# Ternary feed-forward of a fused transformer kernel: transposes moved from TensorE to transposing DMAs, row maxima and rounding two tiles ahead

## The chip, the cores and the metric

The kernel runs on one core of a Trainium2 chip. The metric is the device time of one launch in microseconds (us). The core has a matrix engine (TensorE, PE in the profile), a vector engine (VectorE, DVE), an activation engine (ScalarE, ACT), a general engine (GpSimd, POOL) and a queue that only issues transfers here (SyncE, SP). Each engine runs its own program in order and waits on semaphores.

## The reference, cut to what matters

The whole function is two transformer layers: attention and a ternary feed-forward, then a long convolution and an 8-bit feed-forward. The change touches the ternary feed-forward of layer 0. On the normalised rows `x` (2048 rows of 512) it computes

```python
def _quant_weight(w):
    scale = jnp.mean(jnp.abs(w)) + EPS
    return jnp.clip(jnp.round(w / scale), -1.0, 1.0) * scale
def _quant_act(x):
    scale = jnp.maximum(jnp.max(jnp.abs(x), axis=-1, keepdims=True), EPS) / 127.0
    return jnp.clip(jnp.round(x / scale), -128.0, 127.0) * scale
gate = sigmoid(bitlinear(x, w_gate))      # 512 -> 2048
up = bitlinear(x, w_up)                   # 512 -> 2048
return bitlinear(gate * up, w_down)       # 2048 -> 512
```

where `bitlinear(x, w)` is `_quant_act(x) @ _quant_weight(w).T`. Each row is thus scaled by its own maximum and rounded to whole numbers, once before the first two products and once before the third. The result, times a gate, is added to the residual.

## The kernel before, in words

`phase_bitlinear` (line 880) is one block of the program. It works on 16 tiles of 128 rows, in a loop that is unrolled by `over_tiles`. The weights already lie in memory as bfloat16 whole numbers. A tile `t` goes through these steps:

1. DVE, `prepare` (lines 1063 to 1073): centre and scale the row (`xn`), take its maximum, form the scale and its inverse, multiply and add MAGIC (which rounds), form the gate and up scales, subtract MAGIC into `xq` (bfloat16). This is done for tile t+1 while tile t is worked on.
2. PE, `turn_x` (line 942): four 128x128 transposes of `xq` into PSUM. ACT, `copy_x` (line 998): the copy from PSUM to `xT`.
3. PE, line 976: for each of four chunks c of 512 hidden columns, 4 matmuls for gate and 4 for up, into one of two PSUM buffers `G`. Chunk c waits until the product of chunk c-2 is formed (`h_ready`).
4. ACT, line 1031: sigmoid of the gate half. DVE, line 1123: times the up half, into `h`. DVE, line 1097 (`chunk_max`): the maximum of the chunk.
5. DVE, `quantise` (lines 1086 to 1092), at the head of the next tile: the row's maximum and scales, then `h` times scale plus MAGIC over all 2048 columns. ACT, `round_h` (line 1012): minus MAGIC into `hq` (bfloat16), behind the sigmoid of chunk 1.
6. PE, `turn_h` (line 953): sixteen transposes of `hq`, behind chunk 3 of the next tile. ACT, `copy_h` (line 1004): two copies from PSUM to `hT`.
7. PE, `down` (line 963): 16 matmuls into `D`, for tile t-2, behind chunk 1 of tile t. ACT, `take_down` (line 1019): scaled copy to `ds`. POOL, line 1158: add to the residual `X`. DVE, `row_stats` (line 83): statistics of the new row for the next layer.

Besides, DVE takes the maximum of the next layer's weights (lines 1134 and 1140), a piece of 512 KB in each tile, behind chunk 2; SP loads it (line 930) into one of two buffers. SP also loads the long convolution's context, `ctxT_sb`, in four loads of 1 MB (line 934), ahead of the first tile. That data is not read in this block.

The order on each engine is written out by hand. On PE:

```python
for c in range(NCH):
    if not (first and c < 2):
        pe.wait_ge(h_ready, NCH * t + c - 1)
    ...
    if c == 1 and not early(t):
        down(t - 2, par, same(t, 2))
```

Of the kernel before, what the change touches and what calls it, by code (L numbers as in the profile page):

```python
# [879 lines left out]
def phase_bitlinear(core, ctx, A):  # L880
# [7 lines left out]
    with ExitStack() as free:  # L888
# [3 lines left out]
        def sem(name):  # L892
# [9 lines left out]
        sc = sb("sc_f", [P, 2, 16], F32)  # L902
        AMAX, SX, RX, GS, US, H0, HM, HS, RH, FH, CO = 0, 1, 2, 3, 4, 5, 9, 10, 11, 12, 13
        G = free.enter_context(nc.psum_tensor("ps_g", [P, 2, 2, L], F32))
        XTP = free.enter_context(nc.psum_tensor("ps_xt", [P, 2 * L], BF16))
        HTP = free.enter_context(nc.psum_tensor("ps_ht", [P, 2, 2 * L], BF16))
        D = free.enter_context(nc.psum_tensor("ps_d", [P, L], F32))
        x_step, xq_ready, xt_done, xT_ready = sem("xf_step"), sem("xq_ready"), sem("xt_done"), sem("xT_ready")
        gu_done, sig_ready, h_ready, h_step, ha_ready, hq_ready = (sem(n) for n in (
            "gu_done", "sig_ready", "h_ready", "h_step", "ha_ready", "hq_ready"))  # L910
        ht_done, hT_ready, down_done, xf_updated, scales_ready = (sem(n) for n in (
            "ht_done", "hT_ready", "down_done", "xf_updated", "scales_ready"))
# [10 lines left out]
        with nc.Block() as block:  # L923

            @block.sync
            def _(sp):
                def tile(t, par, first, last):
                    if not early(t):
                        sp.wait_ge(w8m_ready, t - 1)
                    sp.dma_start(w8c[:, par], A["w8"][bass.ds(2 * t, 2)].rearrange("m p l -> p m l"))\  # L930
                        .then_inc(w8c_loaded[par], 16)

                for lt in range(LT):
                    sp.dma_start(core.cT[:, lt], A["ctxT"][lt * P:(lt + 1) * P]).then_inc(core.cT_loaded, 16)
                over_tiles(sp, ROWT, tile)

            @block.tensor
            def _(pe):
                def turn_x(t, par):
                    pe.wait_ge(xq_ready, t + 1)  # L940
                    for lt in range(LT):
                        mm = nc.tensor.transpose(XTP[:, lt * P:(lt + 1) * P], xq[:, par, lt * P:(lt + 1) * P],
                                                 core.ident16[:])
                    mm.then_inc(xt_done, 1)

                def turn_h(t, par, first):
                    pe.wait_ge(hq_ready, t + 1)
                    for half in range(2):
                        if not first:
                            pe.wait_ge(hT_ready, 2 * t + half - 1)  # L950
                        for k in range(KT // 2):
                            c = half * (KT // 2) + k
                            mm = nc.tensor.transpose(HTP[:, half, k * P:(k + 1) * P], hq[:, par, c * P:(c + 1) * P],
                                                     core.ident16[:])
                        mm.then_inc(ht_done, 1)

                def down(t, par, first):
                    if not first:
                        pe.wait_ge(d_taken, t)
                    for half in range(2):  # L960
                        pe.wait_ge(hT_ready, 2 * t + half + 1)
                        for k in range(half * KT // 2, (half + 1) * KT // 2):
                            mm = nc.tensor.matmul(D[:], hT[:, par, k, :], wd[:, k, :], start=(k == 0),  # L963
                                                  stop=(k == KT - 1))
                    mm.then_inc(down_done, 1)

                turn_x(0, 0)

                def tile(t, par, first, last):
                    pe.wait_ge(xT_ready, t + 1)  # L970
                    for c in range(NCH):
# [9 lines left out]
                        if c == 2 and not last:  # L981
                            turn_x(t + 1, 1 - par)
                        if c == 3 and not first:
                            turn_h(t - 1, 1 - par, same(t, 1))
                    if last:
                        down(t - 1, 1 - par, False)
                        turn_h(t, par, False)
                        down(t, par, False)
# [4 lines left out]
            def _(act):  # L993
                ln_scalar(core, act, 1)

                def copy_x(t, par, first):
                    act.wait_ge(xt_done, t + 1)
                    nc.scalar.activation(xT[:, par].rearrange("p a b -> p (a b)"), XTP[:, 0:L], ACT.Copy)\
                        .then_inc(xT_ready, 1)

                def copy_h(t, par):
                    for half in range(2):
                        act.wait_ge(ht_done, 2 * t + half + 1)
                        nc.scalar.activation(hT[:, par, half * KT // 2:(half + 1) * KT // 2, :]  # L1004
                                             .rearrange("p a b -> p (a b)"), HTP[:, half, :], ACT.Copy)\
                            .then_inc(hT_ready, 1)

                def round_h(t, par):
                    act.wait_ge(ha_ready, t + 1)
                    if not early(t):  # L1010
                        act.wait_ge(ht_done, 2 * (t - 1))
                    nc.scalar.activation(hq[:, par, :], h[:, par, :], ACT.Copy, bias=-MAGIC).then_inc(hq_ready, 1)

                def take_down(t, par, first):
# [4 lines left out]
                    nc.scalar.activation(ds[:, 0, :], D[:], ACT.Identity, scale=sc[:, par, CO:CO + 1])\  # L1019
                        .then_inc(d_taken, 1)  # L1020

                copy_x(0, 0, True)

                def tile(t, par, first, last):
                    for c in range(NCH):
# [3 lines left out]
                        if not (first and c < 2):  # L1029
                            act.wait_ge(h_ready, NCH * t + c - 1)  # L1030
                        nc.scalar.activation(sg[:, c % 2, :], G[:, c % 2, 0, :], ACT.Sigmoid,  # L1031
                                             scale=sc[:, par, GS:GS + 1]).then_inc(sig_ready, 1)
                        if c == 1 and not first:
                            round_h(t - 1, 1 - par)
                        if c == 2 and not last:
                            copy_x(t + 1, 1 - par, first)
                        if c == 2 and not early(t):
                            take_down(t - 2, par, same(t, 2))
                        if c == 3 and not first:
                            copy_h(t - 1, 1 - par)  # L1040
                    if last:
                        take_down(t - 1, 1 - par, False)
                        round_h(t, par)
                        copy_h(t, par)
# [5 lines left out]
            def _(dve):  # L1050
                def col(par, c):
                    return sc[:, par, c:c + 1]

                def prepare(t, par, n):
# [3 lines left out]
                    def step(ins):  # L1058
                        ins.then_inc(x_step, 1)
                        steps[0] += 1  # L1060
                        dve.wait_ge(x_step, 6 * n + steps[0])

                    step(nc.vector.tensor_scalar(xn[:, par:par + 1, :], X[:, bass.ds(t, 1), :],
                                                 core.mean[:, bass.ds(t, 1)], core.rstd[:, bass.ds(t, 1)],
                                                 ALU.subtract, ALU.mult))
                    step(nc.vector.tensor_reduce(col(par, AMAX), xn[:, par, :], AX.X, ALU.max,
                                                 apply_absolute_value=True))
                    step(nc.vector.tensor_scalar(col(par, SX), col(par, AMAX), QEPS, 1.0 / 127.0, ALU.max, ALU.mult))
                    step(nc.vector.reciprocal(col(par, RX), col(par, SX)))
                    step(nc.vector.tensor_scalar(xn[:, par, :], xn[:, par, :], col(par, RX), MAGIC, ALU.mult, ALU.add))  # L1070
                    step(nc.vector.tensor_scalar(sc[:, par, GS:US + 1], core.w_scale[:, 0:2], col(par, SX), None,
                                                 ALU.mult))
                    nc.vector.tensor_scalar(xq[:, par, :], xn[:, par, :], -MAGIC, None, ALU.add)\
                        .then_inc(xq_ready, 1)

                def quantise(t, par, n):
# [8 lines left out]
                    dve.wait_ge(hmax_ready, NCH * (t + 1))  # L1085
                    step(nc.vector.tensor_reduce(col(par, HM), sc[:, par, H0:H0 + NCH], AX.X, ALU.max))
                    step(nc.vector.tensor_scalar(col(par, HS), col(par, HM), col(par, US), QEPS, ALU.mult, ALU.max))
                    step(nc.vector.tensor_scalar(col(par, FH), col(par, HS), 1.0 / 127.0, None, ALU.mult))
                    step(nc.vector.reciprocal(col(par, RH), col(par, FH)))
                    step(nc.vector.tensor_tensor(col(par, HS), col(par, RH), col(par, US), ALU.mult))  # L1090
                    step(nc.vector.tensor_tensor(col(par, CO), col(par, FH), core.down_gain, ALU.mult))
                    nc.vector.tensor_scalar(h[:, par, :], h[:, par, :], col(par, HS), MAGIC, ALU.mult, ALU.add)\
                        .then_inc(ha_ready, 1)

                def chunk_max(t, par, c):
                    dve.wait_ge(h_ready, NCH * t + c + 1)
                    nc.vector.tensor_reduce(col(par, H0 + c), h[:, par, c * L:(c + 1) * L], AX.X, ALU.max,
                                            apply_absolute_value=True).then_inc(hmax_ready, 1)

                def statistics(t):  # L1100
                    dve.wait_ge(xf_updated, t + 1)
                    dve.wait_ge(xf_start, 1)
                    row_stats(core, t)

                ln_vector(core, dve, 1)
                nc.vector.tensor_tensor(core.down_gain, core.w_scale[:, 2:3], core.tanh_g[:, 2:3], ALU.mult)\
                    .then_inc(xf_start, 1)
                dve.wait_ge(xf_start, 1)
                prepare(0, 0, 0)

                def tile(t, par, first, last):
                    if first:
                        dve.wait_ge(x_step, 6)

                    nc.vector.tensor_copy(sc[:, par, 14:15], sc[:, par, SX:SX + 1]).then_inc(scales_ready, 1)
                    if not first:
                        quantise(t - 1, 1 - par, t - 1)
                    for c in range(NCH):
# [6 lines left out]
                        if c:  # L1125
                            chunk_max(t, par, c - 1)
# [769 lines left out]
```

## Time and profile before

| | us |
|---|---|
| median of three runs | 1290.32 |
| lowest and highest run | 1289.95, 1292.22 |
| the profiled execution, own time | 1293.39 |
| its span, first to last instruction | 1291.6 |
| PE, DVE, ACT, POOL busy over the span | 1107.0, 1022.1, 669.8, 515.1 |
| the ternary feed-forward in it | 568.8 to 784.5 |

Times inside the span are us from its first instruction. In a timeline each line is a start, a duration, the engine, the source line and the operation; in square brackets stands how long the engine was idle before it and what ended that. PEld is PE's loading of the stationary operand, which goes beside the matmuls. Matmul ends are modelled, so the distance between two starts on PE tells more than a duration. A line "x16" merges sixteen instructions.

### The profile page before, as it was taken

The numbers are of one execution on the slowest core, as the hardware profiler recorded it, in microseconds if no ns is written. First come the engines' busy times: TensorE is split into PE (matmuls) and PEld (weight loads), VectorE is DVE, ScalarE is ACT, GpSimd is POOL, SyncE is SP. The second block draws the span as 40 slices with busy tenths as digits, with TensorE's granted clock in tenths as the row PEclk, the third lists the DMA queues.
The fourth block names the chain that finished last, engine by engine and source line by source line (L and its number), as shares of the span: only waits on it lengthen the run. The fifth ranks groups of instructions, "written<-read, shape, count | busy, mean of one in ns | idle before, by whom it ended". The sixth has DMA issues, their size and how long they took to land. (4 is left out here: it accounts for less than half of the span.)

```text
span 1291.6 us, 13977 instructions
## 1 busy us (share of the span) xinstructions
PE 1107.0 (86%) x4802; PEld 447.7 (35%) x4802; DVE 1022.1 (79%) x1560; ACT 669.8 (52%) x783; POOL 515.1 (40%) x403
## 2 busy tenths in 40 slices
PE   4977869999999999828999985999999998189687
PEld 2533112222222222103444442444444443034232
DVE  5678958888888888219999983887888877777898
ACT  1646047887877877925666662110000000686896
POOL 2756111535435435530011113788887883000021
PEclk8989579999999999969999997999999999599878
DMA  9799933436346444141111101121121120000011
GB/s 323 248 300 332 290 94 98 125 124 198 115 133 189 130 131 131 53 153 65 41 50 49 34 17 37 49 65 49 65 66 51 63 66 17 1 1 1 1 65 65
DMA packets 69319, 131.84 MB, mean 102 GB/s; under 512 B 18048, under 2 KB 35840, under 8 KB 65664
## 3 DMA queue, kind: packets, MB, share of 16 engines
q1 hardware_dynamic: 69248, 130.95, 32.0%
q8 instruction: 38, 0.62, 0.2%
q14 instruction: 33, 0.27, 0.1%
HBM read 106.53 MB, written 22.02 MB: 100 GB/s over the span
## 5 line engine op out<-in xcount | busy, mean ns | idle before, releaser
L797 DVE TENSOR_REDUCE mneg<-ps_m 128x1 f32<-128x512 f32 x512 | 320.0, 683 | 55.4 <-PE ps_m L713 55.0
L1341 PE MATMUL ps_y<-kv,toeplitz_sb 128*128 128x512 f32 x640 | 279.9, 596 | 9.1 <-POOL kv L1253 9.1
L674 ACT ACTIVATE probs<-ps_s 128x1024 f32<-128x1024 f32 x256 | 250.8, 1022 | 45.2 <-PE ps_s L736 45.2
L713 PE MATMUL ps_m<-k_stack,q_stack 112*128 112x512 bf16 x512 | 186.5, 406 | 9.3 <-DMA k_stack<-mask_k 8.7
L1341 PEld LDWEIGHTS ps_y<-kv,toeplitz_sb 128*128 128x128 f32 x640 | 121.2, 192 | 155.6 <-issue 155.6
L736 PE MATMUL ps_s<-q_stack,k_stack 112*128 112x512 bf16 x512 | 153.4, 383 | 22.4 <-DMA q_stack<-mrow 11.7
L746 PE MATMUL ps_o<-probs,v_all 128*17 128x512 f32 x1024 | 134.7, 598 | 0.4 <-ACT probs L674 0.4
L1253 POOL TENSOR_TENSOR kv<-vT,ctxT_sb 128x2048 f32<-128x2048 f32 x32 | 118.8, 3713 | 39.3 <-PE ps_y L1341 32.8
L976 PE MATMUL ps_g<-w,xT_f 128*128 128x512 bf16 x512 | 120.0, 383 | 7.1 <-DVE h_f L1123 6.3
L1407 DVE TENSOR_TENSOR z<-ps_y,ctxT_sb 128x1024 f32<-128x1024 f32 x64 | 78.0, 1218 | 47.5 <-PE ps_y L1341 47.5
L1306 ACT ACTIVATE w_anchor<-w_f 128x512 f32<-128x512 f32 x32 | 20.1, 629 | 180.6 <-DMA w_f<-in_w 180.6
L619 POOL TENSOR_TENSOR inv_all<-inv_all,mb_b 128x512 f32<-128x512 f32 x16 | 20.4, 1275 | 206.0 <-DMA inv_all<-inv_rows 206.0
L713 PEld LDWEIGHTS ps_m<-k_stack,q_stack 112*128 112x128 bf16 x512 | 43.3, 99 | 160.9 <-DVE mneg L797 79.4
L1158 POOL TENSOR_TENSOR X<-X,down_sums 128x512 f32<-128x512 f32 x16 | 20.6, 1286 | 195.2 <-ACT down_sums L1019 195.2
L1664 PE MATMUL ps_fp<-w 128*128 128x512 bf16 x256 | 68.9, 428 | 20.2 <-DVE w L1731 10.1
L1415 DVE TENSOR_REDUCE vT<-z 128x256 f32<-128x2304 f32 x32 | 81.7, 2553 | 1.1
L83 DVE BATCH_NORM_STATS2 bn<-X 128x6 f32<-128x512 f32 x64 | 42.6, 683 | 45.8 <-POOL X L627 21.2
L736 PEld LDWEIGHTS ps_s<-q_stack,k_stack 112*128 112x128 bf16 x512 | 46.2, 98 | 91.5 <-ACT probs L674 32.7
L1031 ACT ACTIVATE sg_f<-ps_g,sc_f 128x512 f32<-128x512 f32 x64 | 43.8, 688 | 56.2 <-PE ps_g L976 38.3
L637 POOL TENSOR_SCALAR w<-w_sweep 128x512 bf16<-128x512 f32 x48 | 70.5, 1491 | 1.3
L976 PEld LDWEIGHTS ps_g<-w,xT_f 128*128 128x128 bf16 x512 | 48.4, 99 | 65.1 <-DVE h_f L1123 10.3
L963 PE MATMUL ps_d<-w,hT_f 128*128 128x512 bf16 x256 | 59.5, 387 | 1.6 <-ACT hT_f L1004 1.6
(159 smaller groups left out, 1614.7 us busy)
## 6 DMA issues: line engine op xcount, KB each, us to landing
w_sweep<-in_w SPq DMA_DIRECT2D x8, 1536.0 KB, 10.3
q_stack<-q_parts SPq DMA_DIRECT2D x96, 128.0 KB, 4.7
k_stack<-k_parts SPq DMA_DIRECT2D x96, 128.0 KB, 4.5
w_sweep<-in_w SPq DMA_DIRECT2D x16, 768.0 KB, 5.3
w_sweep<-in_w SPq DMA_DIRECT2D x16, 512.0 KB, 3.6
toeplitz_sb<-in_toeplitz SPq DMA_DIRECT2D x32, 256.0 KB, 2.6
w_f<-in_w SPq DMA_DIRECT2D x32, 256.0 KB, 2.8
k_parts<-qk_part SPq DMA_DIRECT2D x24, 256.0 KB, 6.2
```

Source lines behind the costliest of these rows:

```text
L637: nc.gpsimd.tensor_scalar(core.w3[:, m].rearrange("p a b -> p (a b)")[:, u * L:(u + 1) * L], wc[:, h, m, :], MAGIC, None, ALU.subtract).th ...
L674: nc.scalar.activation(pr[:, k % 2, 2 * slot:2 * slot + 2, :], S[:, 2 * slot:2 * slot + 2, :], ACT.Exp).then_inc(exp_done, 1)
L713: nc.tensor.matmul(M[:, bank(j), :], Q[slot][0:ROWS, hd, tc * P:(tc + 1) * P], K[slot][0:ROWS, hd, :], start=True, stop=True).then_inc(max ...
L736: mm = nc.tensor.matmul(S[:, g, :], K[slot4][0:ROWS, hd, (k % LT) * P:(k % LT + 1) * P], Q[slot4][0:ROWS, hd, :], start=True, stop=True)
L746: mm = nc.tensor.matmul(O[32 * g:32 * g + HD + 1, :], V[:, par, sc, h * UH + 2 * g + G, :], pr[:, k % 2, g, :], start=(sc == 0), stop=(sc ...
L797: nc.vector.tensor_reduce(mneg[:, h, tile % LT, tile // LT:tile // LT + 1], M[:, bank(j), :], AX.X, ALU.max, negate=True).then_inc(max_red, 1)
L976: mm = nc.tensor.matmul(G[:, c % 2, j, :], xT[:, par, k, :], wt[:, k, c * L:(c + 1) * L], start=(k == 0), stop=(k == LT - 1))
L1253: nc.gpsimd.tensor_tensor(kv[:, g % 2].rearrange("p l (b j i) -> p (l b) j i", b=B, j=GROUP), over_j(group(vT, g)), over_i(group(cT, g)), ...
L1341: mm = nc.tensor.matmul(Y[:, q % 3, l2, :], T[:, g % 2, (lt - m) * P:(lt - m + 1) * P], kv[:, g % 2, m, :], start=(m == 0), stop=(m == lt))
L1407: nc.vector.tensor_tensor(z[:, g % 2, NB // 2 * half:NB // 2 * (half + 1), :, 0:GROUP], Y[:, q % 3].rearrange("p l (b j i) -> p (l b) j i" ...
L1415: nc.vector.tensor_reduce(group(vT, g), z[:, g % 2], AX.X, ALU.add).then_inc(red_ready, 1)
L1664: mm = nc.tensor.matmul(D[:, r, :], h8[:, j % 4, L * t + r * P:L * t + (r + 1) * P], proj[:, ot, :], start=(i == 0 and t == 0), stop=(i == ...
```

## The change

- `turn_x`, `copy_x`, `turn_h` and `copy_h` are gone, with their PSUM buffers. SP issues transposing DMAs from buffer to buffer in SBUF in their place: one of 128x512 bfloat16 (128 KB) for `xq` to `xT`, one of 128x2048 (512 KB) for `hq` to `hT`.
- `prepare` runs two tiles ahead. ACT now centres the row (from a shift `nb` computed once) and does both rounding steps; DVE keeps the maximum and the scales.
- `chunk_max` over 512 columns becomes `half_max` over 1024, twice a tile. The scale columns `sc` have four sets in place of two, and the copy that published them (line 1115) is gone.
- On ACT, `round_h` moves from behind the sigmoid of chunk 1 to behind that of chunk 2, `take_down` from chunk 2 to chunk 3. On DVE the next layer's weight maximum moves from chunk 2 to chunk 1, and the statistics are those of tile t-3 in place of t-2.
- The four loads of `ctxT_sb` move from ahead of the first tile to the end of SP's part of tile 0.

The core of the diff:

```diff
 SP
+                def turn_x(t, par):
+                    sp.wait_ge(xq_ready, t + 1)
+                    if t >= 2:
+                        sp.wait_ge(gu_done, NCH * (t - 1))
+                    sp.dma_start(xT[:, par], xq[:, par, :], transpose=True).then_inc(xT_ready[par], 16)
+                def turn_h(t, par):
+                    sp.wait_ge(hq_ready, t + 1)
+                    if t >= 2:
+                        sp.wait_ge(down_done, t - 1)
+                    sp.dma_start(hT[:, par], hq[:, par, :], transpose=True).then_inc(hT_ready[par], 16)
                 def tile(t, par, first, last):
                     if not early(t):
                         sp.wait_ge(w8m_ready, t - 1)
                     sp.dma_start(w8c[:, par], A["w8"][bass.ds(2 * t, 2)].rearrange("m p l -> p m l"))\
                         .then_inc(w8c_loaded[par], 16)
-
-                for lt in range(LT):
-                    sp.dma_start(core.cT[:, lt], A["ctxT"][lt * P:(lt + 1) * P]).then_inc(core.cT_loaded, 16)
+                    if not first:
+                        turn_h(t - 1, 1 - par)
+                    if t + 2 < ROWT:
+                        turn_x(t + 2, par)
+                    if first:
+                        for lt in range(LT):
+                            sp.dma_start(core.cT[:, lt], A["ctxT"][lt * P:(lt + 1) * P]).then_inc(core.cT_loaded, 16)
+                    if last:
+                        turn_h(t, par)
+
+                turn_x(0, 0)
+                turn_x(1, 1)
 PE
-                    for half in range(2):
-                        pe.wait_ge(hT_ready, 2 * t + half + 1)
-                        for k in range(half * KT // 2, (half + 1) * KT // 2):
-                            ...
+                    pe.wait_ge(hT_ready[par], 16 * (t // 2 + 1))
+                    for k in range(KT):
+                        mm = nc.tensor.matmul(D[:], hT[:, par, k, :], wd[:, k, :], start=(k == 0), stop=(k == KT - 1))
...
-                        if c == 2 and not last:
-                            turn_x(t + 1, 1 - par)
-                        if c == 3 and not first:
-                            turn_h(t - 1, 1 - par, same(t, 1))
 ACT
+                def centre(t, par):
+                    nc.scalar.activation(xn[:, par, :], X[:, t, :], ACT.Identity, bias=nb[:, t:t + 1],
+                                         scale=core.rstd[:, t:t + 1]).then_inc(xn_ready, 1)
+                def round_x(t, par):
+                    act.wait_ge(rx_ready, t + 1)
+                    nc.scalar.activation(xn[:, par, :], xn[:, par, :], ACT.Identity, bias=core.magic,
+                                         scale=sc[:, t % 4, RX:RX + 1]).then_inc(xr_ready, 1)
+                    act.wait_ge(xr_ready, t + 1)
+                    if t >= 2:
+                        act.wait_ge(xT_ready[par], 16 * (t // 2))
+                    nc.scalar.activation(xq[:, par, :], xn[:, par, :], ACT.Copy, bias=-MAGIC).then_inc(xq_ready, 1)
...
-                        if c == 1 and not first:
+                        if c == 1 and t + 2 < ROWT:
+                            round_x(t + 2, par)
+                        if c == 2 and not first:
                             round_h(t - 1, 1 - par)
-                        if c == 2 and not last:
-                            copy_x(t + 1, 1 - par, first)
-                        if c == 2 and not early(t):
+                        if c == 3 and t + 3 < ROWT:
+                            centre(t + 3, 1 - par)
+                        if c == 3 and not early(t):
                             take_down(t - 2, par, same(t, 2))
-                        if c == 3 and not first:
-                            copy_h(t - 1, 1 - par)
 DVE
+                    dve.wait_ge(xn_ready, t + 1)
+                    step(nc.vector.tensor_reduce(col(t, AMAX), xn[:, par, :], AX.X, ALU.max,
                                                  apply_absolute_value=True))
+                    step(nc.vector.tensor_scalar(col(t, SX), col(t, AMAX), QEPS, 1.0 / 127.0, ALU.max, ALU.mult))
+                    nc.vector.reciprocal(col(t, RX), col(t, SX)).then_inc(rx_ready, 1)
+                    nc.vector.tensor_scalar(sc[:, t % 4, GS:US + 1], core.w_scale[:, 0:2], col(t, SX), None, ALU.mult)\
+                        .then_inc(scales_ready, 1)
...
-                        if c:
-                            chunk_max(t, par, c - 1)
-                        if c == 0 and not last:
-                            if not first:
-                                dve.wait_ge(xt_done, t)
-                            prepare(t + 1, 1 - par, t + 1)
                         if c == 2:
+                            half_max(t, par, 0)
+                        if c == 0 and t + 2 < ROWT:
+                            prepare(t + 2, par, t + 2)
+                        if c == 1:
                             dve.wait_ge(w8c_loaded[par], 8 * (t - par) + 16)
...
-                        if c == 3 and not early(t):
-                            statistics(t - 2)
-                    chunk_max(t, par, NCH - 1)
+                        if c == 3 and t >= 3:
+                            statistics(t - 3)
+                    half_max(t, par, 1)
```

## Rows read from the trace of the kernel before

**Rows 1.** Busy time by stretch: first tiles, a steady tile, the end.

```profile
core 0: us, PE busy (x) PEld busy (x) DVE busy (x) ACT busy (x) POOL busy (x), PEclk, DMA share, GB/s
582.00:594.00 12.00, 8.39 (x41) 3.32 (x39) 11.51 (x27) 4.84 (x6) 0.00 (x0) 1.00 0.23 79
654.00:666.00 12.00, 11.79 (x70) 5.71 (x68) 11.55 (x27) 7.53 (x10) 1.28 (x1) 1.00 0.13 44
774.00:786.00 12.00, 6.37 (x32) 2.82 (x32) 2.10 (x9) 4.21 (x5) 1.26 (x1) 0.86 0.01 4
```

**Rows 2.** Timeline of a steady tile: TensorE and its partners, in program order.

```profile
657.91 1.09 PEld L953 LDWEIGHTS ps_ht<-ident,hq_f 128*128 128x128 bf16 x16
658.91 1.93 ACT L1004 ACTIVATE hT_f<-ps_ht 128x1024 bf16<-128x1024 bf16 x2
658.97 3.17 PEld L976 LDWEIGHTS ps_g<-w,xT_f 128*128 128x128 bf16 x16
662.47 3.62 PE L963 MATMUL ps_d<-w,hT_f 128*128 128x512 bf16 x16
664.39 1.91 ACT L1012 ACTIVATE hq_f<-h_f 128x2048 bf16<-128x2048 f32 x1 [1.03 <-DVE h_f L1092]
665.93 1.89 PE L976 MATMUL ps_g<-w,xT_f 128*128 128x512 bf16 x8
667.86 0.69 ACT L1031 ACTIVATE sg_f<-ps_g,sc_f 128x512 f32<-128x512 f32 x1 [1.55 <-PE ps_g L976]
668.44 0.59 ACT L998 ACTIVATE xT_f<-ps_xt 128x512 bf16<-128x512 bf16 x1
669.94 1.09 PEld L953 LDWEIGHTS ps_ht<-ident,hq_f 128*128 128x128 bf16 x16
```

**Rows 3.** The same timeline, DVE's `prepare` and what borders on it.

```profile
664.87 0.54 DVE L1063 TENSOR_SCALAR xn_f<-X,mean,rstd 128x512 f32<-128x512 f32 x1
665.45 0.69 DVE L1066 TENSOR_REDUCE sc_f<-xn_f 128x1 f32<-128x512 f32 x1
666.17 0.15 DVE L1068 TENSOR_SCALAR sc_f<-sc_f 128x1 f32<-128x1 f32 x1
667.08 0.23 DVE L1071 TENSOR_SCALAR sc_f<-columns,sc_f 128x2 f32<-128x2 f32 x1
667.68 0.68 DVE L1123 TENSOR_TENSOR h_f<-sg_f,ps_g 128x512 f32<-128x512 f32 x1
```

**Rows 4.** Timeline of the first tile.

```profile
568.81 1.98 SPq L934 DMA_DIRECT2D ctxT_sb<-in_ctxT  x4
570.89 0.16 DVE L1106 TENSOR_TENSOR columns<-columns,tanh_g 128x1 f32<-128x1 f32 x1
575.34 5.24 PE L976 MATMUL ps_g<-w,xT_f 128*128 128x512 bf16 x16 [0.69 <-ACT xT_f L998]
586.74 1.21 DVE L1134 TENSOR_REDUCE w_max_t<-w_sweep 128x2 f32<-128x1024 f32 x1
587.03 0.69 ACT L1031 ACTIVATE sg_f<-ps_g,sc_f 128x512 f32<-128x512 f32 x1 [1.50 <-PE ps_g L976]
```

**Rows 5.** Timeline of the last tile.

```profile
776.18 5.30 PE L963 MATMUL ps_d<-w,hT_f 128*128 128x512 bf16 x16 [0.76 <-ACT hT_f L1004]
782.29 1.26 POOL L1158 TENSOR_TENSOR X<-X,down_sums 128x512 f32<-128x512 f32 x1 [8.81 <-ACT down_sums L1019]
783.58 0.69 DVE L83 BATCH_NORM_STATS2 bn<-X 128x6 f32<-128x512 f32 x1 [9.38 <-POOL X L1158]
```

**Rows 6.** DMA issues: size of each, median us from issue to landing.

```profile
w_sweep<-in_w SPq DMA_DIRECT2D x16, 512.0 KB, 3.6
k_parts<-qk_part SPq DMA_DIRECT2D x24, 256.0 KB, 6.2
v_rows<-vp SPq DMA_DIRECT2D x8, 544.0 KB, 10.5
out<-X SPq DMA_DIRECT2D x16, 256.0 KB, 2.0
num<-odd_heads SPq DMA_DIRECT2D x64, 32.0 KB, 1.9
```

**Rows 7.** Line 930, the weight pieces: least, median, longest landing.

```profile
DMA to landing us min/median/max: 3.5/3.6/13.0
```

More of the change, by code:

```diff
@@ L938, in _ @@
             def _(pe):
[L939 to L947, printed above, removed]
-                    for half in range(2):
-                        if not first:
[L950 to L955, printed above, removed]
                 def down(t, par, first):
@@ L959, in down @@
                         pe.wait_ge(d_taken, t)
-                    for half in range(2):
-                        pe.wait_ge(hT_ready, 2 * t + half + 1)
-                        for k in range(half * KT // 2, (half + 1) * KT // 2):
-                            mm = nc.tensor.matmul(D[:], hT[:, par, k, :], wd[:, k, :], start=(k == 0),
-                                                  stop=(k == KT - 1))
+                    pe.wait_ge(hT_ready[par], 16 * (t // 2 + 1))
+                    for k in range(KT):
+                        mm = nc.tensor.matmul(D[:], hT[:, par, k, :], wd[:, k, :], start=(k == 0), stop=(k == KT - 1))
                     mm.then_inc(down_done, 1)
-                turn_x(0, 0)
                 def tile(t, par, first, last):
-                    pe.wait_ge(xT_ready, t + 1)
+                    pe.wait_ge(xT_ready[par], 16 * (t // 2 + 1))
                     for c in range(NCH):
@@ L994, in _ @@
                 ln_scalar(core, act, 1)
[L996 to L1006, printed above, removed]
+                act.wait_ge(xf_start, 1)
+                def centre(t, par):
[9 more added lines that the diff above has]
+                    nc.scalar.activation(xq[:, par, :], xn[:, par, :], ACT.Copy, bias=-MAGIC).then_inc(xq_ready, 1)
+                centre(0, 0)
+                centre(1, 1)
+                round_x(0, 0)
+                round_x(1, 1)
+                centre(2, 0)
                 def round_h(t, par):
@@ L1018, in take_down @@
                         act.wait_ge(xf_updated, t)
-                    nc.scalar.activation(ds[:, 0, :], D[:], ACT.Identity, scale=sc[:, par, CO:CO + 1])\
+                    nc.scalar.activation(ds[:, 0, :], D[:], ACT.Identity, scale=sc[:, t % 4, CO:CO + 1])\
                         .then_inc(d_taken, 1)
-                copy_x(0, 0, True)
                 def tile(t, par, first, last):
@@ L1043, in tile @@
                         round_h(t, par)
-                        copy_h(t, par)
                         take_down(t, par, False)
@@ L1154, in tile, with update @@
                 def tile(t, par, first, last):
+                    if not early(t):
+                        update(t - 2)
+                    if last:
+                        update(t - 1)
+                        update(t)
+                def update(t):
                     pool.wait_ge(d_taken, t + 1)
-                    pool.wait_ge(xf_start, 1)
+                    pool.wait_ge(xf_start, 2)
                     xt = X[:, bass.ds(t, 1), :]
```

70 lines of the change are left out of this document (30 added, 40 removed).

## The prediction

> **What bounds the kernel now.** I read first the busy times by stretch. In a steady stretch of 12 us of this phase PE is busy 11.79 us and DVE 11.55 us [rows 1]; ACT (7.5) and POOL (1.3) have room. Two engines are thus near their limit, and a table of shares can't tell which one paces. The timeline can. One tile lasts 12.03 us, from one block of `hq` transposes to the next (657.91 to 669.94) [rows 2]. PE starts 16 matmuls of 512 columns 3.46 us apart (662.47 to 665.93) [rows 2], so its 48 matmuls of a tile need 3 x 3.46 = 10.4 us. The sixteen `hq` transposes take 1.06 us more (657.91 to 658.97), the four of `xq` some 0.25 us: 11.7 us in all. DVE has no gap: its instructions follow each other to the next tile, and the sigmoid of chunk 2 finds its PSUM ready while PE had waited for DVE. So DVE paces, with PE 0.3 us behind it. Both must be relieved, and the change relieves both.
>
> **DVE.** `prepare` lasts 2.81 us (664.87 to 667.68) [rows 3]. Of it remain the maximum (0.72 from start to start, 665.45 to 666.17), the scale and the reciprocal (0.2 each, by the first of them), and the scale pair (0.23): 1.35 us. The copy of line 1115 (0.12) goes too. Two maxima over 1024 columns replace four over 512; line 1134 reduces 1024 columns in 1.21 us [rows 4], which is two of the old ones (0.6 apart), so nothing is gained. DVE: 12.03 - 1.46 - 0.12 = 10.45 us.
>
> **PE.** 10.4 us, without transposes.
>
> **ACT.** It loses copies of 1.93 and 0.59 us [rows 2] and gains a centring and two roundings of 512 columns, 0.69 us each at most by the sigmoid's row [rows 2]: 2.1 us. Its load stays at 7.5 us. What changes is its order, and this matters below.
>
> If nothing else held, a tile would take 10.45 us and the phase would save 16 x 1.6 = 25 us. **But the order closes a new loop.** `hq` of tile t is rounded behind the sigmoid of chunk 2 of tile t+1, on ACT. The DMA may start then, and `down` of tile t stands on PE behind chunk 1 of tile t+2. Before, the rounding stood one chunk earlier. Chunk 2 of tile t+2, whose sigmoid precedes the next rounding, stands on PE behind this `down`. So from one `down` to the next: the 16 matmuls 3.46 us (662.47 to 665.93), chunk 2 until its sigmoid starts 1.93 us (665.93 to 667.86), the sigmoid 0.69, `round_h` 1.91 [rows 2], then the transfer with SP's wake-up and issue, which I call D. A tile can't be shorter than **8.0 + D**. It equals the old 12.03 at D = 4.0. PE, meanwhile, has only chunk 3, chunk 0 and chunk 1 (5.2 us) to do between the start of that rounding's sigmoid and `down`; the sigmoid, rounding and D exceed that.
>
> **What is D?** The trace before has no transposing DMA. For the same bytes, the 512 KB weight piece lands 3.6 us after its issue [rows 6]. From below: 256 KB out of SBUF takes 2.0 us and 32 KB from SBUF to SBUF 1.9 [rows 6]; so 512 KB within SBUF could hardly land before 2.5 us, if turning were free. From above: 544 KB out of SBUF takes 10.5 us in a crowded queue [rows 6]. Between them stands the row nearest in kind, bfloat16 rows out of SBUF in short pieces: 256 KB in 6.2 us, in part queued. A transposition also has to be cut in more pieces than a copy of whole rows. I take D = 5.0, about halfway between the plain copy's 3.6 and that 6.2, and keep 2.5 and 10.5 as ends.
>
> The Trainium skill ("Advanced Engine Details and Errata", section X-Bar Transpose (TRN2)) says that transposing DMAs are as fast as regular ones. No row here shows it. By that rule D would be the 3.6 us of the weight piece, and the sum below would come to 1295.
>
> **The transfer of x** (128 KB) is off the path: it is issued right behind that of h, and is wanted a tile later. It delays the weight piece behind it on SP, which has until chunk 1. The semaphore that frees `hq` is `hT_ready` from then on; two buffers cover it.
>
> **The start.** Before, the first gate matmul starts 4.45 us after the last setup instruction on DVE (570.89 to 575.34) [rows 4]. After: shift 0.2, centring 0.7, maximum and scales 1.1, two roundings 1.4, a transfer of 128 KB of some 2.5 (by the 1.9 and 2.0 of [rows 6]), 5.9 us. So +1.5 us.
>
> **The context loads** (4 MB) now stand behind tile 0, where SP waits for the last gate matmul of tile 0 (before at 587.0, its sigmoid starting at 587.03 [rows 4]; the later start and the shorter `prepare` cancel, so some 588 after). Before, the first weight piece, issued behind them, took 13.0 us [rows 7], and landed at 583.8, 15.0 us after their first issue at 568.81 [rows 4]. It was wanted only at 586.74, so it cost nothing. Now the piece of tile 1 lands at 588.1 + 15.0 = 603.1, while DVE wants it behind chunk 1 of tile 1, about 595. Behind it on DVE: its maximum 1.3, the product of chunk 2 0.6, `half_max` 1.2, the product of chunk 3 0.7, then chunk 1 of tile 2 on PE 1.73, then `down(0)`, at 608.7. Without this hold it would be at 600 + D (`hq` of tile 0 rounded about 600) = 605: the hold costs nearly 4 us. Its cover, the old place ahead of the first tile, is gone.
>
> **The end.** From `down(14)`: its matmuls 3.6, `take_down` 0.7, `round_h(15)` 1.9, D, the last `down` 5.3 at the lower clock, then 0.7 + 1.3 + 0.7 and handovers [rows 5]: 14.5 + D.
>
> **The sum**, for D = 5.0: 608.7 + 14 x 13.0 + 14.5 + 5.0 = 810.2, where the phase's last statistics ended at 784.3 (783.58 + 0.69) [rows 5]. That is +26 us. The profiled execution took 1293.39 us, 3.1 over the median of 1290.32; I take the difference to the median: **1316**. In general the end is at 608.7 + 126.5 + 15 D; it breaks even at D = 3.3, and each 0.1 us of D is worth 1.5 us.
>
> **Rivals.**
>
> *A quick transfer* (faster). If D is below 3.3, ACT's order bounds: sigmoid 2, `round_h` 1.91, sigmoid 3, the product, chunk 1 on PE, `down` and chunk 2: 0.69 + 1.91 + 0.73 + 0.75 + 1.73 + 3.46 + 1.93 = 11.2, with waits 11.3 us a tile. With D = 2.5 and the context's hold hidden after all, the end is at 602.5 + 14 x 11.3 + 14.5 + 2.5 = 777.7, or 6.6 us sooner: 1284. For it: the two rows at 1.9 and 2.0 us [rows 6], and a queue that is free (DMA share 0.13 [rows 1]). Against: those move less, and untransposed. Chance 0.16.
>
> *A draw*: D between 2.7 and 3.5, with the hold: 1288 to 1293. Chance 0.11.
>
> *The blocks go one after another.* `hT` is sixteen 128x128 blocks of 32 KB; a 32 KB transfer takes 1.9 us [rows 6], so D would be up to 30 us and the time 1290 + (600 + 30 + 14 x 38.4 + 45 - 784) = 1719. PE turned these sixteen in 1.06 us, which speaks against moving them. The same would follow if the transposition went element by element. Nothing in the trace excludes it. Chance 0.04.
>
> The Trainium skill ("VectorE: DVE Perf Modes", section The three transpose paths) gives 1309 ns for one 128x128 block by DMA, against 390 ns on TensorE. Sixteen such one by one would make D 21 us and the time about 1567; side by side, nothing.
>
> *PE's clock falls* in the gaps of 2.6 us that each tile gets. In the stretch 582 to 594 PE is busy 8.39 of 12 us with the clock at 1.00, in the last one 6.37 with 0.86 [rows 1]. The loop's `down` at the lower clock takes 5.3 in place of 3.6 us: with chunk 2, 2.6 us a tile, 14 x 2.6 = 36 more: 1353. Chance 0.03, within slower.
>
> **Chances.** The loop with D from 3.5 to 8 (1293 to 1361) has 0.55; with D from 8 to 10.5 (to 1399) 0.11; the two rare cases 0.07. The likeliest case's own range is 1293 to 1361. The whole range goes from the quick transfer to D at 10.5: 1284 to 1398. A difference of 0.2% (2.6 us) is about what a measurement of this kernel can tell. Faster 0.16, same 0.11, slower 0.73.
>
> **What would show it.** Right: `down` (PE, 16 matmuls) idle before it by 2 to 3 us, ended by the DMA into `hT_f`; a period of 8.0 us plus the landing time of that DMA; DVE and ACT idle several us a tile; in tile 1 DVE idle some 8 us for `w_sweep`. Wrong: `down` starting right behind chunk 1 (then D is below 3.3, and the period 11.3 or less), a period paced by `ps_g`, or no wait for `w_sweep` in tile 1. If PEclk falls below 1.00 in steady tiles, the clock's case is in play.

## Result and profile after

| | before | changed |
|---|---|---|
| median of 4 runs, us | 1290.72 | 1302.47 |
| lowest to highest | 1289.95 to 1292.22 | 1300.21 to 1303.24 |
| ratio to before, 95% interval | | 1.0087 [1.0069, 1.0104] |
| span of the profiled execution | 1291.6 | 1298.4 |

The change made the kernel 11.8 us slower. The direction was forecast, the size was not: +26 us were named, 1316 against 1302.5.

The two profiled spans differ by less (6.8 us), because the attention ahead of this phase ended 4.0 us sooner in the second profile: DVE's first instruction behind it (line 104) starts at 564.87 and not at 568.85. That part of the code is the same. So I measure the phase from this instruction to the same one of the next phase: 568.85 to 784.60 before, 564.87 to 791.25 after, 215.8 and 226.4 us. **The phase is 10.6 us longer**, and that is the change.

The timeline of a steady tile of the changed kernel, to be held against [rows 2, 3]:

```profile
700.19 3.61 PE L968 MATMUL ps_d<-w,hT_f 128*128 128x512 bf16 x16 [0.55 <-DMA hT_f<-hq_f]
703.64 5.37 PE L978 MATMUL ps_g<-w,xT_f 128*128 128x512 bf16 x24
705.57 0.69 ACT L1036 ACTIVATE sg_f<-ps_g,sc_f 128x512 f32<-128x512 f32 x1 [0.54 <-PE ps_g L978]
706.15 1.90 ACT L1019 ACTIVATE hq_f<-h_f 128x2048 bf16<-128x2048 f32 x1
707.95 0.68 ACT L1036 ACTIVATE sg_f<-ps_g,sc_f 128x512 f32<-128x512 f32 x1
708.08 1.63 SPq L940 DMA_TRANSPOSE hT_f<-hq_f  x1
709.41 1.90 PE L978 MATMUL ps_g<-w,xT_f 128*128 128x512 bf16 x8 [0.40 <-DVE h_f L1122]
709.81 1.22 SPq L933 DMA_TRANSPOSE xT_f<-xq_f  x1
711.89 3.61 PE L968 MATMUL ps_d<-w,hT_f 128*128 128x512 bf16 x16 [0.58 <-DMA hT_f<-hq_f]
```

Read it as a ring. `down` 700.19, chunk 2 703.64, its sigmoid 705.57, `round_h` 706.15, done at 708.05, transfer issued 708.08, next `down` 711.89. The legs are 3.45, 1.93, 0.58, 1.90 and 3.84: 11.70 us. PE waits for the DMA ahead of `down`, as forecast, but only 0.55 us. Before it stands a second wait, for DVE's product of chunk 3, 0.40 us on PE: ACT takes that chunk's sigmoid (707.95) only after `round_h`.

The landing times of the same kernel over the phase (size of the plain ones, median us from issue to landing):

```profile
w_sweep<-in_w SPq DMA_DIRECT2D x15, 512.0 KB, 3.8
hT_f<-hq_f SPq DMA_TRANSPOSE x16, 3.7
xT_f<-xq_f SPq DMA_TRANSPOSE x14, 2.4
```

So D, from `hq` ready to `down`, is 3.8 us and not 5.0. The busy times by stretch of the changed kernel, as in [rows 1]:

```profile
core 0: us, PE busy (x) PEld busy (x) DVE busy (x) ACT busy (x) POOL busy (x), PEclk, DMA share, GB/s
594.00:606.00 12.00, 4.79 (x14) 1.77 (x15) 6.64 (x13) 2.22 (x4) 0.00 (x0) 0.72 0.73 220
654.00:666.00 12.00, 11.05 (x51) 4.63 (x50) 10.35 (x21) 7.05 (x9) 1.27 (x1) 1.00 0.40 108
762.00:774.00 12.00, 7.41 (x27) 2.78 (x25) 8.01 (x15) 3.64 (x4) 1.26 (x1) 0.79 0.19 44
```

In the steady stretch neither PE nor DVE is full any more. The two ends are where the time is lost. The first, in tile 1 (the context loads, and the wait they cause):

```profile
584.49 2.39 SPq L953 DMA_DIRECT2D ctxT_sb<-in_ctxT  x4
586.92 0.45 SPq L945 DMA_DIRECT2D w_sweep<-in_w  x1
590.40 0.68 DVE L1122 TENSOR_TENSOR h_f<-sg_f,ps_g 128x512 f32<-128x512 f32 x1
594.28 4.64 SPq L940 DMA_TRANSPOSE hT_f<-hq_f  x1
599.05 1.22 DVE L1130 TENSOR_REDUCE w_max_t<-w_sweep 128x2 f32<-128x1024 f32 x1 [7.97 <-DMA w_sweep<-in_w]
601.21 5.58 PE L978 MATMUL ps_g<-w,xT_f 128*128 128x512 bf16 x16 [8.14 <-DVE h_f L1122]
606.63 3.62 PE L968 MATMUL ps_d<-w,hT_f 128*128 128x512 bf16 x16
```

DVE stands 7.97 us for the weight piece, PE then 8.14 for DVE, and its next 16 matmuls take 5.42 us (601.21 to 606.63) instead of 3.45: the granted clock of that stretch is 0.72, a mixture of the two levels. The second, behind the last tile:

```profile
770.29 6.37 PE L968 MATMUL ps_d<-w,hT_f 128*128 128x512 bf16 x16 [4.59 <-DMA hT_f<-hq_f]
777.28 1.90 ACT L1019 ACTIVATE hq_f<-h_f 128x2048 bf16<-128x2048 f32 x1
783.00 5.15 PE L968 MATMUL ps_d<-w,hT_f 128*128 128x512 bf16 x16 [6.34 <-DMA hT_f<-hq_f]
790.24 0.69 DVE L83 BATCH_NORM_STATS2 bn<-X 128x6 f32<-128x512 f32 x1 [10.79 <-POOL X L1163]
```

From `down(14)` to the end of the last statistics: 20.6 us. Before, it was 16.7 (767.59 to 784.27). `down(0)` and `down(14)` of the kernel before:

```profile
602.62 3.62 PE L963 MATMUL ps_d<-w,hT_f 128*128 128x512 bf16 x16
767.59 3.61 PE L963 MATMUL ps_d<-w,hT_f 128*128 128x512 bf16 x16 [0.89 <-ACT hT_f L1004]
```

Against these two starts the 10.6 us come apart: 8.0 are there by `down(0)` (it starts 33.8 us into the phase before, 41.8 after), the fourteen tiles from `down(0)` to `down(14)` give 1.3 back (165.0 before, 163.7 after), and 4.0 come behind `down(14)` (17.0 before, 21.0 after, to the next phase).

### The profile page after: what moved, and what is told of

It is laid out like the page before. It is cut to its first block and busy times, and to the rows that moved or that the text cites. A ratio compares the mean times of both kernels' runs of the same rounds, so it can differ in the third digit from the quotient of the medians.

```text
span 1298.4 us, 13318 instructions
## 1 busy us (share of the span) xinstructions
PE 1093.5 (84%) x4482; PEld 429.7 (33%) x4482; DVE 997.3 (77%) x1465; ACT 661.4 (51%) x783; POOL 514.3 (40%) x403
## 2 busy tenths in 40 slices
DMA packets 111300, 142.29 MB, mean 110 GB/s; under 512 B 60032, under 2 KB 77824, under 8 KB 107648
## 5 line engine op out<-in xcount | busy, mean ns | idle before, releaser
L736 PE MATMUL ps_s<-q_stack,k_stack 112*128 112x512 bf16 x512 | 153.3, 383 | 20.5 <-ACT probs L674 10.4
L1669 PE MATMUL ps_fp<-w 128*128 128x512 bf16 x256 | 66.9, 417 | 22.3 <-DVE w L1736 11.8
L968 PE MATMUL ps_d<-w,hT_f 128*128 128x512 bf16 x256 | 62.1, 399 | 18.4 <-DMA hT_f<-hq_f 18.4
L1122 DVE TENSOR_TENSOR h_f<-sg_f,ps_g 128x512 f32<-128x512 f32 x64 | 43.6, 684 | 30.6 <-ACT sg_f L1036 30.5
```

The source lines that it names most:

```text
L736: mm = nc.tensor.matmul(S[:, g, :], K[slot4][0:ROWS, hd, (k % LT) * P:(k % LT + 1) * P], Q[slot4][0:ROWS, hd, :], start=True, stop=True)
L1669: mm = nc.tensor.matmul(D[:, r, :], h8[:, j % 4, L * t + r * P:L * t + (r + 1) * P], proj[:, ot, :], start=(i == 0 and t == 0), stop=(i == ...
```

## The experiments

Theory: three separate costs. A ring through `down`, the rounding and the transfer sets a tile at 7.86 + D; the context loads, late in the queue, hold DVE in tile 1; the end has two transfers in series. Rivals: the rate of the transposing DMAs or one of the engines sets the tile; the hold and the end are hidden or come from other causes. Each kernel was timed beside the kernel before: 1290.7 us beside the changed kernel, 1291.1 beside runs 1 to 4, 1291.8 beside runs 5 to 8, so a difference between two groups carries about 1 us of doubt. "Phase" is the distance defined above, in the one profiled execution of each kernel.

| kernel | median us | ratio to before, 95% | phase us | a steady tile us |
|---|---|---|---|---|
| before | | | 215.8 | 12.03 |
| changed | 1302.47 | 1.0087 [1.0069, 1.0104] | 226.4 | 11.7 |
| 1, context loads earlier | 1293.43 | 1.0022 [1.0012, 1.0032] | 218.1 | 11.7 |
| 2, round_h first | 1281.60 | 0.9924 [0.9911, 0.9937] | 205.8 | 10.5 |
| 3, last rounding first | 1294.69 | 1.0027 [1.0016, 1.0039] | 219.5 | 11.7 |
| 4, h in two halves | 1292.26 | 1.0006 [0.9994, 1.0017] | 215.5 | 11.0 |
| 5, before, context late | 1294.73 | 1.0018 [1.0003, 1.0032] | 219.1 | 12.0 |
| 6, edits 1 to 3 together | 1272.02 | 0.9848 [0.9817, 0.9878] | 195.3 | 10.5 |
| 7, edit 2, h on TensorE | 1288.76 | 0.9981 [0.9967, 0.9996] | 213.7 | 11.25 |
| 8, one more transfer | 1323.30 | 1.0249 [1.0221, 1.0277] | 249.2 | 13.0 |

**1. The context loads earlier.**

```diff
+                    if first:
+                        for lt in range(LT):
+                            sp.dma_start(core.cT[:, lt], ...)
                     if not first:
                         turn_h(t - 1, 1 - par)
                     if t + 2 < ROWT:
                         turn_x(t + 2, par)
-                    if first:
-                        for lt in range(LT):
-                            sp.dma_start(core.cT[:, lt], ...)
```

> The changed kernel with the four context loads issued right behind the first weight piece, ahead of the x transfer of tile 2. Theory (the hold): their 4 MB land by about 587 and the weight piece of tile 1 by about 590, just before DVE wants it at 591; the 7.97 us that DVE stood in tile 1 go, and with them the fall of PE's clock behind it. down(0) can start at about 599 in place of 606.6, so the kernel is 6 to 8 us faster than the changed one (about 1295); steady tiles keep 11.7 us. Rival (the hold is hidden, because the loop through down would have set the pace anyway): within 1 us of the changed kernel.

Measured: 9.0 us faster than the changed kernel, somewhat more than the 6 to 8 expected, and a phase 8.3 us shorter. `down(0)` starts 33.2 us into the phase and not 41.8. The timeline of this kernel's DVE in tile 1 has no wait ahead of line 1130:

```profile
591.26 0.68 DVE L1122 TENSOR_TENSOR h_f<-sg_f,ps_g 128x512 f32<-128x512 f32 x1
591.86 1.21 DVE L1130 TENSOR_REDUCE w_max_t<-w_sweep 128x2 f32<-128x1024 f32 x1
```

The hold is a cost of its own: the ring does not hide it, because the ring only starts with `down(0)`.

**2. `round_h` ahead of `down`.**

```diff
-                        if c == 1 and t + 2 < ROWT:
-                            round_x(t + 2, par)
-                        if c == 2 and not first:
-                            round_h(t - 1, 1 - par)
+                        if c == 1 and not first:
+                            round_h(t - 1, 1 - par)
+                        if c == 2 and t + 2 < ROWT:
+                            round_x(t + 2, par)
```

> The changed kernel with round_h behind the sigmoid of chunk 1 and round_x behind that of chunk 2 (ACT's two steps swapped, nothing else). Theory (the loop down, chunk 2, sigmoid, round_h, transfer, down): the rounding now stands ahead of a down on PE, so the transfer has chunk 2, 3, 0 and 1 and a down to hide behind; the 3.8 us leave the path and a tile takes 10.5 to 10.8 us instead of 11.7: 14 to 17 us faster than the changed kernel (about 1287), with no wait of PE for the DMA in steady tiles. Rival (the transfers' own rate, or DVE, sets the 11.7): unchanged, 1302.

Measured: 20.9 us faster than the changed kernel, more than the 14 to 17 expected, and 0.76% faster than the one before. The same two engines, the same transfers, two steps swapped:

```profile
672.86 3.62 PE L968 MATMUL ps_d<-w,hT_f 128*128 128x512 bf16 x16
675.36 1.91 ACT L1019 ACTIVATE hq_f<-h_f 128x2048 bf16<-128x2048 f32 x1 [1.62 <-DVE h_f L1092]
676.31 7.23 PE L978 MATMUL ps_g<-w,xT_f 128*128 128x512 bf16 x32
677.30 1.32 SPq L940 DMA_TRANSPOSE hT_f<-hq_f  x1
683.38 2.97 PE L968 MATMUL ps_d<-w,hT_f 128*128 128x512 bf16 x13
```

`round_h` now runs beside `down` of the tile before, and the 32 matmuls between two `down` cover the transfer, issued at 677.30 and first needed at 683.38. A tile is 10.52 us (672.86 to 683.38). From `down(0)` to `down(14)` it is 145.1 us (609.7 to 754.8) where it was 163.7 (606.6 to 770.3), and the end is 2.4 us shorter: `down(14)` comes right behind the copy of `down(13)` and takes 3.63 us, not 6.4. These two make 21.0 us; 0.4 go the other way ahead of `down(0)`, where the hold of the context loads grew: DVE waited 8.91 us for the weight piece and not 7.97. With those loads in flight SP also stood 9.08 us over the issue of `turn_h`:

```profile
593.27 9.08 SPq L940 DMA_TRANSPOSE hT_f<-hq_f  x1
602.50 1.22 DVE L1130 TENSOR_REDUCE w_max_t<-w_sweep 128x2 f32<-128x1024 f32 x1 [8.91 <-DMA w_sweep<-in_w]
```

**3. The last rounding ahead of the copy of `down(14)`.**

```diff
                     if last:
-                        take_down(t - 1, 1 - par, False)
                         round_h(t, par)
+                        take_down(t - 1, 1 - par, False)
                         take_down(t, par, False)
```

> The changed kernel with, behind the last tile, the rounding of tile 15 ahead of the copy of down(14) on ACT. Theory (the end costs a second full transfer in series): hq of tile 15 is ready at about 774 in place of 779.2, its transfer lands before down(14) ends, and the last down starts some 6 us sooner, at 777: 5 to 6 us faster than the changed kernel (about 1297). Rival (the end is paced by the matmuls at the lower clock): under 2 us.

Measured: 7.8 us faster than the changed kernel, a phase 6.9 us shorter, somewhat more than the 5 to 6 expected. The gain is the transfer that no longer stands in series, and the last `down` at the full clock: 3.61 us instead of 5.15, behind an idle time of 1.53 us on PE and not of 6.34.

```profile
769.11 5.97 PE L968 MATMUL ps_d<-w,hT_f 128*128 128x512 bf16 x16 [4.59 <-DMA hT_f<-hq_f]
770.90 1.91 ACT L1019 ACTIVATE hq_f<-h_f 128x2048 bf16<-128x2048 f32 x1 [4.44 <-DVE h_f L1092]
775.11 0.69 ACT L1026 ACTIVATE down_sums<-ps_d,sc_f 128x512 f32<-128x512 f32 x1 [2.30 <-PE ps_d L968]
776.61 3.61 PE L968 MATMUL ps_d<-w,hT_f 128*128 128x512 bf16 x16 [1.53 <-DMA hT_f<-hq_f]
```

**4. The transfer of h in two halves.**

```diff
-                    sp.dma_start(hT[:, par], hq[:, par, :], transpose=True).then_inc(hT_ready[par], 16)
+                    for half, done in enumerate((hT_first, hT_ready)):
+                        sp.dma_start(hT[:, par, half * KT // 2:(half + 1) * KT // 2],
+                                     hq[:, par, half * FF // 2:(half + 1) * FF // 2], transpose=True)\
+                            .then_inc(done[par], 16)
```

`down` waits for `hT_first`, and for `hT_ready` ahead of its ninth matmul.

> The changed kernel with the transfer of h in two of 256 KB, each with its own semaphore; down starts on the first. Theory (the transfer is a fixed part plus a part by bytes; 128 KB took 2.4 us and 512 KB 3.7 from issue to landing, so 256 KB should take 2.8): down starts 0.9 us sooner in each tile, until ACT's order bounds (sigmoid 2, round_h, sigmoid 3, product, chunk 1, down, chunk 2: 10.95 us): a tile takes about 11.0 and the kernel is 9 to 11 us faster than the changed one (about 1292). Rival (the duration is all fixed, or each transfer is served whole after the other): no gain, or slower by the second issue, 1302 to 1310.

Measured: 10.2 us faster than the changed kernel; no different from the kernel before. The medians of the halves and of x, and `down` without a wait for the DMA:

```profile
hT_f<-hq_f SPq DMA_TRANSPOSE x28, 2.8
xT_f<-xq_f SPq DMA_TRANSPOSE x13, 2.3
```

```profile
672.76 1.90 PE L983 MATMUL ps_g<-w,xT_f 128*128 128x512 bf16 x8 [0.40 <-DVE h_f L1128]
674.78 3.61 PE L973 MATMUL ps_d<-w,hT_f 128*128 128x512 bf16 x16
```

128, 256 and 512 KB land in 2.3 to 2.4, 2.8 and 3.7 us. The statistics of successive tiles start at 740.02, 751.05 and 762.01: 11.0 us a tile, the bound by ACT's order that stands in the expectation. Four of the fourteen tiles take 11.3 to 11.6 us; in three of them DVE waits 1.0 to 1.3 us for the weight piece (to 646.91, 702.78 and 736.36), which stands on SP behind the transposing DMAs.

**5. The late context loads alone, in the kernel before.**

```diff
-                for lt in range(LT):
-                    sp.dma_start(core.cT[:, lt], ...)
 ...
+                    if first:
+                        sp.wait_ge(gu_done, NCH)
+                        for lt in range(LT):
+                            sp.dma_start(core.cT[:, lt], ...)
```

> The kernel before the change with one part of it alone: the four context loads behind tile 0 (SP waits for its last gate matmul, then issues them, then the weight piece of tile 1). Theory (the hold comes from the place of the loads, not from the transposing DMAs): they go out at about 587, the weight piece of tile 1 lands at about 602.4 and DVE wanted it at 598.2, so DVE stands 4 us in tile 1; with a little of PE at the lower clock behind that, 4 to 6 us slower than the kernel before (1295 to 1297). Steady tiles keep 12.03 us. Rival (the hold needs the transposing transfers in the queue): within 1 us of before.

Measured: 2.9 us slower in the median, 3.3 in the phase; a little less than the 4 to 6 expected. The weight piece came at 600.2, two us earlier than reckoned:

```profile
600.23 1.22 DVE L1136 TENSOR_REDUCE w_max_t<-w_sweep 128x2 f32<-128x1024 f32 x1 [1.87 <-DMA w_sweep<-in_w]
```

So the place of the loads costs time without any transposing DMA, though the interval only just excludes zero (0.4 to 4.1 us). By `down(14)` this phase is 2.3 us behind that of the kernel before. DVE's wait is 1.87 us of it. Ahead of it PE's chunk 1 of tile 1 ran at the lower clock, which it did not in the kernel before:

```profile
592.79 3.52 PE L978 MATMUL ps_g<-w,xT_f 128*128 128x512 bf16 x8 [2.42 <-DVE h_f L1125]
777.89 6.54 PE L965 MATMUL ps_d<-w,hT_f 128*128 128x512 bf16 x16 [0.76 <-ACT hT_f L1006]
```

The last 1.0 us come at the end, where the last `down` took 6.54 us and not 5.30 [rows 5], with the same idle time before it; nothing ties that to the place of the loads.

It costs more in the changed kernel (8.3 us by run 1): DVE wants the piece behind chunk 1 there and not behind chunk 2, and stands 7.97 us for it.

**6. Edits 1, 2 and 3 together.**

> The changed kernel with the three edits together: context loads right behind the first weight piece, round_h behind the sigmoid of chunk 1 and round_x behind that of chunk 2, and the last tile's rounding ahead of the copy of down(14). Theory (the hold of tile 1 and the loop through down are two separate costs, the third edit is worth nothing once the loop is gone, since the rounding of tile 15 then finds its data no earlier): phase 8 us shorter than with the second edit alone (205.8 us), about 197.5, and 1272 to 1275 us in all. Rival (the costs cover each other): about 1281.

Measured: 1272.0 us, **1.5% faster than the kernel before**. The phase is 10.5 us shorter than with edit 2 alone, not 8. The third edit is worth nothing here, as expected: from `down(14)` to the last `down` it is 10.1 us in both (754.80 to 764.90 with edit 2 alone, 745.10 to 755.23 with all three). The whole difference is there by `down(0)`, which starts 31.6 us into the phase (600.02 less 568.46) and not 42.2 (609.73 less 567.54). It is more than the 8.6 us that edit 1 gave alone, for two reasons: the hold was 0.4 us longer under edit 2, and with `hq` of tile 0 rounded earlier `down(0)` no longer waits for its transfer, so it starts 1.6 us sooner than in run 1 (33.2).

**7. h on TensorE, x by DMA, in the order of edit 2.** `turn_h` stands behind chunk 3 on PE and the two copies behind `take_down` on ACT, as in the kernel before.

> The changed kernel in the order of the second edit (round_h behind chunk 1), but with h transposed on TensorE as before (sixteen transposes behind chunk 3, two copies on ACT) and only x by DMA. Theory (once the transfer is off the loop, PE bounds at 10.5 us a tile, and the sixteen transposes come on top in full): 1.06 us more a tile, 11.5 to 11.7 us, so 14 to 17 us slower than the same order with the DMA in the fourteen steady tiles, less 2 to 5 us at the end where the path by TensorE is shorter: 1291 to 1297. Rival (DVE at 10.45 us bounds, and PE has room for them): 1282 to 1285.

Measured: 7.2 us slower than run 2 in the median and 7.9 in the phase, where 10 to 15 were expected. The busy times of this kernel and, below, of run 2:

```profile
678.00:690.00 12.00, 11.95 (x68) 5.90 (x68) 10.75 (x22) 9.48 (x13) 1.27 (x1) 1.00 0.22 67
```

```profile
678.00:690.00 12.00, 12.00 (x56) 5.23 (x55) 11.48 (x23) 8.29 (x11) 1.27 (x1) 1.00 0.48 121
```

With the transposes PE bounds at 11.25 us a tile: 3 x 3.46 us of matmuls and 0.87 for the transposes. Without them PE needs 10.38, but the tile is 10.52: DVE is next. So moving the transposes of h pays 0.73 us a tile and not all that they take. (They take 0.87 us on PE here; the 1.06 of the prediction and of the expectation is the distance on PEld, 657.91 to 658.97.) The expectation had both bounds and subtracted from the wrong one.

**8. One more transfer in the ring.**

```diff
+                        sp.wait_ge(spare_ready[par], 16 * (t // 2))
+                    sp.dma_start(spare[:, par], hq[:, par, 0:L], transpose=True).then_inc(spare_ready[par], 16)
                     sp.dma_start(hT[:, par], hq[:, par, :], transpose=True).then_inc(hT_ready[par], 16)
```

> The changed kernel with one more transposing DMA of 128 KB (a quarter of hq into a spare buffer that nothing reads) issued ahead of that of h in every tile. Theory (the transfer lies in the loop, so every us of it lengthens a tile by one): its issue takes SP 1.2 us and its bytes come first, so D rises from 3.8 to 5.0 or 5.2, a tile from 11.7 to about 13.0, and the kernel is 17 to 22 us slower than the changed one: about 1322. Rival (the loop isn't paced by the transfer; or both are in flight side by side): within 3 us of the changed kernel.

Measured: 1323.3, 20.8 us over the changed kernel. D and the tile rise together, by 1.3 us; the last row is the one steady tile in which the clock fell:

```profile
679.60 1.90 ACT L1026 ACTIVATE hq_f<-h_f 128x2048 bf16<-128x2048 f32 x1
681.52 1.20 SPq L943 DMA_TRANSPOSE spare_f<-hq_f  x1
682.76 1.71 SPq L944 DMA_TRANSPOSE hT_f<-hq_f  x1
686.64 3.61 PE L974 MATMUL ps_d<-w,hT_f 128*128 128x512 bf16 x16 [1.88 <-DMA hT_f<-hq_f]
713.12 5.30 PE L974 MATMUL ps_d<-w,hT_f 128*128 128x512 bf16 x16 [2.30 <-DMA hT_f<-hq_f]
```

D is 5.1 us here (681.50 to 686.64), which happens to be near the value of the prediction, and the time is 1323 where the prediction said 1316 for 5.0. The tile of the last row took 14.67 us and not 13.0.

## Why the prediction was right in kind and wrong in size

- **The ring, 8.0 + D a tile: right.** 3.45 + 1.93 + 0.58 + 1.90 = 7.86, and two values of D lie on it: 3.84 gives 11.70, and 5.1 gives 13.0 (run 8). Broken open, it leaves DVE's bound (run 2).
- **D = 5.0: this is the step that failed.** It measured 3.8. I set it halfway between the 3.6 us of a plain load of 512 KB and the 6.2 us of 256 KB of bfloat16 rows, on the ground that turned data goes in more pieces. The 6.2 is a median over transfers that landed in anything from 2.1 to 10.5 us: the 48 out of `qk_part`, all of 256 KB and of the same form, in the trace of the kernel before. So most of it was not size or kind, and the crowd in the queue is the likely rest. In the prediction I wrote "in part queued" and gave it half the weight all the same. The Trainium skill's rule ("Advanced Engine Details and Errata", section X-Bar Transpose (TRN2)) that transposing DMAs are as fast as regular ones agrees with this trace: 3.7 us beside the 3.8 of the plain 512 KB. This term alone is 15 x (5.0 - 3.8) = 18 us too much, more than the whole miss of 14 us (1316 against 1302.5).
- **The two rare rivals: out for the changed kernel.** Sixteen blocks one after another were put at up to 30 us; 512 KB land in 3.7 us. The clock stayed at 1.00 through the gaps of its steady tiles, which are about 1 us and not the 2.6 foreseen. With longer gaps the rival is not empty: in run 8, whose tiles last the 13.0 us of the prediction, the clock fell in one of fourteen, which cost 1.7 us.
- **The context loads, some 4 us: the mechanism was right, the size too small.** Run 1 gives 8.3 to 9.0. DVE was forecast idle some 8 us there and was, 7.97. The landing was forecast about 32 us behind DVE's last setup instruction (603.1 less 571.05) and came there (599.05 less 567.14 is 31.9). What I left out is PE at the lower clock behind its idle time, 2.0 us (5.42 less 3.45). And the alternative, `down(0)` at 605, was set too late: by 1.2 us for D, and by 1.7 because `hq` of tile 0 is ready 29.4 us into the phase (run 1, transfer issued at 595.13, phase from 565.70) and not 31.2. 3.7 + 2.0 + 1.2 + 1.7 is 8.6, which is what `down(0)` gained in run 1 (41.8 less 33.2).
- **The end, 14.5 + D: 18.3 with the measured D; it was 20.6.** Again the clock: `down(14)` had waited 4.59 us for its transfer and took 6.4 us, 2.8 more than I gave it. (One profile: in that of run 1 the same wait of 4.6 us was followed by a `down` of 5.2 us, and the last one took 6.2.) I had put the clock's fall down as a rival in the steady tiles, where it did not happen, and for the last `down`; I had left it out behind the wait in tile 1 and at `down(14)`, where my own working left PE idle for several us too.
- **The start, +1.5 us: right.** From DVE's last setup instruction to the first gate matmul it is 6.1 us (566.99 to 573.11), before 4.45: +1.7.
- **The sum again** with what was measured: -18 for D, -2 for the ring's other legs, +2 and +2.3 for the clock at the two ends, from +26: +10.3. The phase is 10.6 longer.
- **DVE at 10.45 us a tile and PE at 10.4: right,** though the changed kernel never shows it. Run 2 does: 10.52. In the kernel before, PE had 0.5 us of room and not 0.3, since the transposes of `hq` take 0.89 us on PE there (658.13 to 659.02) and not 1.06. The change had the gain that its parts promise; the order on ACT took it back.

## What to carry to other kernels

When a step on a fast path is replaced by a slower one that runs beside the engines, follow its result round the ring: what waits for it, what stands behind that in program order, and whether the next input of the same step stands there. Here a transfer of 3.8 us cost nothing ahead of 32 matmuls and 1.2 us a tile when its producer stood behind its own consumer; swapping two activations on ACT was worth 21 us. A load that nobody needs yet is not free either: it has to go where the next wanted load has slack, and where PE will idle for several us, its next matmuls are to be costed at the lower clock too.

## What the runs showed of the hardware

- A transposing DMA from SBUF to SBUF lands 2.4 us after issue for 128 KB, 2.8 for 256 KB and 3.7 for 512 KB: about 1.3 us for 384 KB more. At 512 KB that is the pace of the plain transfer beside it (3.8), although it is cut small: the page of the changed kernel counts 60032 packets under 512 bytes, that of the kernel before 18048.
- Its issue holds SP longer than that of a plain DMA, 1.6 us for 512 KB and 1.2 for 128 KB against 0.57 for the plain 512 KB beside it (0.37 in the kernel before). With the 4 MB of context in flight, one issue took 4.64 us (594.28 above), and 9.08 in run 2.
- The clock: after 8.1 and 4.6 us of idleness PE's next matmuls ran at the lower level at first, 5.4 and 6.4 us for sixteen in place of 3.45. After the 1.9 us of most tiles in run 8 they did not, after 2.30 us in one of them they did (713.12 to 718.26, 5.1 us for sixteen; the granted clock from 713 to 716 was 0.53). One wait alone doesn't decide it: chunk 1 of tile 1 follows a wait of 2.4 us on DVE in run 5 and in the changed kernel (589.44), and only in run 5 did its matmuls run at the lower level (8 in 3.36 us, 592.79 to 596.15; 16 in 3.63 us there).
